# Expert weights in 4 KB pieces, with transposes that pick every fourth (second) column

## The chip, the cores and the metric

One core of one Trainium2 chip runs the whole program. The metric is the device time of one execution in microseconds (us). Lower is better.

## The reference, cut to what matters

A block of 2048 tokens with width H = 512 passes through a time-mixing and channel-mixing layer, and then through a mixture of experts. The change touches the routed experts alone:

```python
E, I = (32, 256)          # 32 experts, inner width 256; H = 512
...
_, topk_idx = jax.lax.top_k(sfc_masked, K)      # K = 4 experts for each token
...
up = jnp.einsum('th,ehi->tei', h, Wu)           # Wu: (32, 512, 256), float32
act = _relu2(up)                                # relu, then squared
routed = jnp.einsum('tei,te,eih->th', act, combine, Wd)   # Wd: (32, 256, 512), float32
shared = _relu2(h @ Wsu) @ Wsd
out = (routed + shared).reshape(orig_shape)
```

The two routed products sum over H (512) and over I (256). A sum may be cut into groups of 128 terms in any way, if both factors are cut in the same way.

## The kernel before, in words

The program has five stages. Stages 1 and 2 are the attention-like layer and its channel mixing, stage 3 the shared expert and the routing, stage 4 the routed experts, and stage 5 the rest of the shared expert and the final sum. All semaphores, buffers and the order of the work on each engine are written out by hand.

**Stage 4** works through slots of 128 tokens that are sorted by expert ("tiles"); this input fills 84 of them. The loop runs over passes of GROUP = 12 tiles, with two tiles in flight (u is the tile's number modulo 2). For a tile:

- GpSimd (POOL) gathers the 128 token rows, 544 floats each, from h_d into a ring of 12 tiles xg (`gather`, L1714).
- TensorE transposes the first 512 columns of xg in four pieces of 128 into PSUM (`tin`, L1535). The tile xg is the stationary operand (weight load) and the 128x128 identity the moving one. ScalarE copies the result to xT4 (L1608).
- TensorE computes the up product (`up`, L1543): four float32 matmuls, each of which sums over 128 of the 512 rows of Wu. Piece c of xT4 meets columns c*256 to (c+1)*256 of wu8, the expert's Wu in SBUF. Each of the four runs in two parts, so there are 8 records for a tile.
- ScalarE applies relu into a4 (L1613), VectorE squares it (L1678), and TensorE transposes it in two pieces of 128 columns (`turn`, L1551). It is split into a high and a low part (L1618, L1682).
- TensorE computes the down product in six fp32r matmuls of 512 columns (`down`, L1558 by way of `split_product`, recorded as L614). The weights for it, wds, are split into high and low from wd8 by ScalarE (`w_hi`, L1624) and VectorE (`w_lo`, L1687), column by column in the order in which they lie.
- ScalarE scales the result into a ring of four tiles yo (`take_y`, L1631), and GpSimd adds its rows by an indirect, accumulating DMA to res_d (even tiles) or shx_d (odd tiles) in HBM (`add_rows`, L1735).

The order on TensorE within a step is: up of tile g, tin of tile g+2, turn of tile g-1, down of tile g-2.

**Waits of the row adds.** `add_rows` for tile g waits until the add of tile g-2, into the same array, has landed. `take_y` for tile g waits until the add of tile g-4, whose ring slot it reuses, has landed. GpSimd issues in the order add, gather, add, gather. So an add that lands late holds GpSimd and then ScalarE, and through ScalarE TensorE.

**Expert weights.** A ring of eight slots, w8, holds one expert each: 1024 floats of Wu and 1024 floats of Wd per partition. SyncE issues two DMAs of 512 KB for an expert (`load`, L1256 and L1258) as soon as the slot is free, that is when the previous owner's last down product is done (`stage4_sync`, L1789 to L1792). The first eight experts are loaded in stage 3. Partition p of the Wu slot holds rows p, 128+p, 256+p and 384+p (four pieces of 1 KB in HBM), and partition p of the Wd slot rows p and 128+p (two pieces of 2 KB). After the last expert SyncE loads hT3, 2 MB with 16 KB for each partition (L1797), for stage 5. SyncE's transfers are on queue q1, those of GpSimd on queue q0, and both share the same 16 DMA engines.

Of the kernel before, what the change touches and what calls it, by code (L numbers as in the profile page):

```python
# [24 lines left out]
P = 128  # L25
T, H = 2048, 512
# [4 lines left out]
C = H // P  # L31
# [4 lines left out]
E, EI, TOPK, GROUPS = 32, 256, 4, 4  # L36
# [37 lines left out]
def program(nc, a, out, scratch):  # L74
# [4 lines left out]
    def sem(name):  # L79
        if name not in sem_names:  # L80
            sem_names[name] = ctx.enter_context(nc.semaphore(name))
        return sem_names[name]

    def at(name, shape, dt, kb):

        return nc.alloc_sbuf_tensor_at(name, shape, dt, offset=SBUF0 + int(kb * KB))

    with ctx:
# [13 lines left out]
        ident = at("ident", [P, P], F, 200.5)  # L102
# [98 lines left out]
        wu8, wd8 = w8[:, :, 0:C * EI], w8[:, :, C * EI:]  # L201
        XRING, YRING = 12, 4
        xg = [at(f"xg{n}", [P, H + E], F, 2.125 * (n % 6) + (186 if n < 6 else 80)) for n in range(XRING)]
        xT4 = at("xT4", [P, 2, C * P], F, 180.5)
        a4 = at("a4", [P, 2, EI], F, 92.75)
# [10 lines left out]
        bank = [ctx.enter_context(nc.psum_tensor(f"bank{i}", [P, 512], F)) for i in range(8)]  # L216
# [392 lines left out]
        def split_product(dst, lhs, rhs, n):  # L609

            parts = [(0, 0), (0, 1), (1, 0)]
            for c in range(n):
                for k, (l, r) in enumerate(parts):
                    i = nc.tensor.matmul(dst, lhs(l, c), rhs(r, c), start=c == 0 and k == 0,  # L614
                                         stop=c == n - 1 and k == 2)
            return i
# [631 lines left out]
        def sp_hTb(sp, b):  # L1248
            sp.dma_start(hTb[:, b % 2].bitcast(F), hT_d[b]).then_inc(sem("hb_in"), 16)

        wu_rows = a["L0_ffn_Wu"].rearrange("e (c p) i -> e p c i", p=P)
        wd_rows = a["L0_ffn_Wd"].rearrange("e (c p) i -> e p c i", p=P)

        def load(sp, e, s):

            sp.dma_start(wu8[:, s].rearrange("p (c n) -> p c n", c=C),  # L1256
                         wu_rows[bass.ds(e, 1)].rearrange("a p c i -> p (a c) i")).then_inc(sem(f"w4_in{s % 4}"), 16)
            sp.dma_start(wd8[:, s].rearrange("p (c n) -> p c n", n=H),  # L1258
                         wd_rows[bass.ds(e, 1)].rearrange("a p c i -> p (a c) i")).then_inc(sem(f"w4_in{s % 4}"), 16)

        def landed(sp, r, s):

# [3 lines left out]
        def first_experts(sp):  # L1266
            sp.wait_ge(sem("wsu_lo1"), 2)
            sp.wait_ge(sem("wsd_lo1"), 2)
            sp.wait_ge(sem("lg_in"), NB)
            sp.wait_ge(sem("xp_st"), 16 * NB)  # L1270
            for s in range(4):
                load(sp, s, s)

        def second_experts(sp):
            for s in range(4):
                landed(sp, 0, s)
            for s in range(4, WSLOTS - 1):
                load(sp, s, s)

        def eighth_expert(sp):  # L1280
            sp.wait_ge(sem("rows_in"), 1)
            sp.wait_ge(sem("share_st"), 16)
            load(sp, WSLOTS - 1, WSLOTS - 1)
# [203 lines left out]
        def passes_of(engine):  # L1487

            return engine.value_load(passes_i[0:1, 0:1], min_val=E // GROUP - 1, max_val=PASSES - 1)
# [3 lines left out]
        def owners(engine, g, n=GROUP):  # L1496

            for k in range(n):
                if k % PACK == 0:
                    word = engine.value_load(owner_i[0:1, bass.ds(g + k, 1)], min_val=0,  # L1500
                                             max_val=(1 << OWNER_BITS * PACK) - 1)
                yield k, (word >> OWNER_BITS * (k % PACK)) & E - 1
# [10 lines left out]
        def x_count(i, t):  # L1513

            return 16 * i + 16 * (t // XRING) + 16

        def first_owners(engine, n):
            return [e for _, e in owners(engine, 0, n)]

        def slot_of(ring, e):  # L1520
            return ring[:, bass.ds(e & WSLOTS - 1, 1)].rearrange("p a n -> p (a n)")

        def up3(pe, i):
            pe_inner_up(pe, N4 + i, i, wsu, lambda s, c: hT3[:, s, c], kc=6)

        def down3(pe, i):
            pe_inner_down(pe, N4 + i, i, NSI - 1, lambda s: wsd[s][:, i], to=2)

        def stage4_tensor(pe, down2):
            def tin(i, t, u):  # L1530
                s = t % XRING
                pe.wait_ge(sem(f"xg_in{s}"), x_count(i, t))
                pe.wait_ge(sem("xt4"), GROUP * i + t + 1)
                for c in range(C):
                    m = nc.tensor.transpose(bank[6 + u][:, c * P:(c + 1) * P], xg[s][:, c * P:(c + 1) * P], ident[:])  # L1535
                m.then_inc(sem("t4"), 1)

            def up(g, u, e):
                pe.wait_ge(sem("win"), e + 1)
                pe.wait_ge(sem("xt4"), g + 3)  # L1540
                pe.wait_ge(sem("r4"), g + 1)
                for c in range(C):
                    m = nc.tensor.matmul(bank[4 + u][:, 0:EI], xT4[:, u, c * P:(c + 1) * P],  # L1543
                                         slot_of(wu8[:, :, c * EI:(c + 1) * EI], e), start=c == 0, stop=c == C - 1)
                m.then_inc(sem("u4"), 1)

            def turn(g, u):
                pe.wait_ge(sem("s4"), g + 1)
                pe.wait_ge(sem("al4"), g + 1)
                for c in range(EI // P):  # L1550
                    m = nc.tensor.transpose(bank[2 + u][:, c * P:(c + 1) * P], a4[:, u, c * P:(c + 1) * P], ident[:])  # L1551
                m.then_inc(sem("at4"), 1)

            def down(g, u):
                pe.wait_ge(sem("al4"), g + 3)
                pe.wait_ge(sem("wl4"), g + 1)
                pe.wait_ge(sem("y4"), g + 1)
                split_product(bank[u][:], lambda s, c: aT4[:, u, s, c * P:(c + 1) * P],  # L1558
                              lambda s, c: wds[:, u, s, c * H:(c + 1) * H], EI // P).then_inc(sem("d4"), 1)

            def step(i, t, e, more=True):
                g, u = GROUP * i + t, t % 2
                up(g, u, e)
                if more:
                    tin(i, t + 2, u)
                turn(g - 1, 1 - u)
                down(g - 2, u)

            down2(NSI - 2)
            pe.wait_ge(sem("owner_in"), 1)  # L1570
            passes = passes_of(pe)
            early = first_owners(pe, 2)
            pe.wait_ge(sem("rows_in"), 1)
            tin(0, 0, 0)
            tin(0, 1, 1)
            down2(NSI - 1)
            pe.wait_ge(sem("kc_free"), N4 + 2)
            up(0, 0, early[0])
            tin(0, 2, 0)
            up(1, 1, early[1])  # L1580
            tin(0, 3, 1)
            pe.wait_ge(sem("sh_in"), (NB - 2) * BT + 1)
            turn(0, 0)
            pe.wait_ge(sem("sh_in"), (NB - 1) * BT)
            with pe.Fori(0, PASSES - 1) as i, pe.If(i < passes):
                for k, e in owners(pe, GROUP * i + 2):
                    step(i, 2 + k, e)
            n = GROUP - 2
            for k, e in owners(pe, GROUP * passes + 2, n):
                step(passes, 2 + k, e, more=k < n - 2)  # L1590
            final = GROUP * passes + GROUP - 1
            pe.wait_ge(sem("hb_in"), 16 * NB)
            turn(final, 1)
            up3(pe, 0)
            down(final - 1, 0)
            up3(pe, 1)
            down(final, 1)
            for i in range(2, NSI):
                up3(pe, i)
                down3(pe, i - 2)  # L1600
            down3(pe, NSI - 2)
            down3(pe, NSI - 1)
# [292 lines left out]
```

## Time and profile before

| | us |
|---|---|
| median of 3 runs (1082.77 to 1088.84) | 1088.8 |
| the profiled execution | 1089.09 |
| its span, first to last instruction | 1086.9 |
| TensorE busy in the span | 1048.4 (96%) |
| first to last up product of stage 4 | 709.4 to 1034.3 |

The profiled execution is one of its own, 0.3 us above the median; 2.2 us of it lie outside the span. In the profile PE is TensorE's matmuls, PEld its weight loads, which run beside the matmul before them, DVE is VectorE, ACT ScalarE, POOL GpSimd and SPq SyncE's queue of instructions. L1543 is line 1543 of the kernel. The ends of matmuls are modelled, so the time from one start to the next says more than the duration of one. A row of the timeline gives the start, the time from the first start to the last end, the engine and line, and the count.

### The profile page before, as it was taken

What the parts mean: (1) busy time and instruction counts of PE and PEld (TensorE: products, weight loads), DVE (VectorE), ACT (ScalarE), POOL (GpSimd) and SP (SyncE); (2) the same over time, 40 slices, a digit from 0 to 9 for tenths busy, and PEclk for the clock granted to TensorE, in tenths of its full rate; (3) what the DMA queues carried; (4) which work ended last, traced back from release to release, by engine and by line L of the source; (5) the groups of instructions that cost most, each with busy time, mean ns of one, the idle gap of its engine ahead of it and who ended that gap; (6) DMA issues with size and microseconds to landing.
All of it is one profiled execution on the core that took longest, in us unless ns stands there. A gap on an engine that the chain in (4) does not pass through costs nothing.

```text
span 1086.9 us, 17057 instructions
## 1 busy us (share of the span) xinstructions
PE 1048.4 (96%) x4868; PEld 841.1 (77%) x4869; DVE 573.4 (53%) x1113; ACT 535.1 (49%) x893; POOL 436.9 (40%) x327
## 2 busy tenths in 40 slices
PE   2999999999999999999999999999999999999998
PEld 0446888888788878887887788888878888887887
DVE  7978947804661475230034796845444444544514
ACT  4644546333333333343344333367767576766742
POOL 1011304221321122112224424467777777887642
PEclk9999999999999999999999999999999999999999
DMA  8705296416422642334266771277989999986678
GB/s 278 265 1 194 86 335 209 166 59 249 155 98 66 224 154 96 116 118 151 90 223 228 259 220 39 68 189 149 279 182 241 254 225 312 199 197 118 87 182 337
DMA packets 98307, 192.91 MB, mean 177 GB/s; under 512 B 13001, under 2 KB 33481, under 8 KB 97745
## 3 DMA queue, kind: packets, MB, share of 16 engines
q1 hardware_dynamic: 79008, 151.63, 40.0%
q0 software_dynamic: 18816, 39.87, 19.6%
q10 hardware_dynamic: 432, 0.79, 0.2%
q8 instruction: 27, 0.44, 0.2%
q14 instruction: 24, 0.19, 0.1%
HBM read 137.78 MB, written 60.03 MB: 182 GB/s over the span
## 4 chain that ended last, share of the span: by engine, by line
PE 75%; DMA 11%; DVE 7%; issue 3%; POOL 2%; SPq 1%; ACT 1%; ACTq 0%; DVEq 0%; POOLq 0%
PE bank L614 35%; PE bank L939 21%; PE bank L1543 8%; DMA shx_d<-yo,idy 6%; PE bank L529 5%; DMA res_d<-yo,idy 3%; PE bank L1535 2%; DVE big L1328 1%; PE bank L1551 1%; DMA hT_d<-hT 1%; SPq L1062 1%; DMA g1b<-in_L_attn_ln_b 1%; PE bank L950 1%; PE bank L1007 1%; PE bank L960 0%
## 5 line engine op out<-in xcount | busy, mean ns | idle before, releaser
L920 POOL TENSOR_TENSOR ksp_lo<-ra,ksp_hi 128x512 fp32r<-128x512 f32 x96 | 148.3, 1545 | 443.0 <-ACT ksp_hi L870 442.9
L1687 DVE TENSOR_TENSOR wds<-w,wds 128x1024 fp32r<-128x1024 f32 x84 | 103.0, 1226 | 167.1 <-ACT wds L1624 167.1
L1543 PE MATMUL bank<-w,xT 128*128 x672 | 159.4, 380 | 1.2 <-ACT xT L1608 0.8
L939 PE MATMUL bank<-vring,ksp_hi 128*128 128x512 f32 x512 | 159.3, 393 | 0.0
L862 ACT ACTIVATE ra<-bank 128x512 f32<-128x512 f32 x96 | 57.4, 597 | 178.2 <-PE bank L614 175.9
L1543 PEld LDWEIGHTS bank<-w,xT 128*128 128x128 f32 x672 | 127.5, 190 | 21.8 <-issue 1.8
L614 PE MATMUL bank<-wds,aT 128*128 128x512 f32 x504 | 138.4, 410 | 0.1
L870 ACT ACTIVATE ksp_hi<-ra 128x512 fp32r<-128x512 f32 x96 | 60.7, 632 | 124.7 <-PE bank L939 124.2
L939 PEld LDWEIGHTS bank<-vring,ksp_hi 128*128 128x128 f32 x512 | 95.5, 188 | 20.1
L1631 ACT ACTIVATE yo<-bank,xg 128x512 f32<-128x512 f32 x84 | 57.8, 688 | 93.1 <-PE bank L614 48.5
L614 PEld LDWEIGHTS bank<-wds,aT 128*128 128x128 f32 x504 | 89.0, 190 | 17.3 <-issue 0.3
L614 PE MATMUL bank<-xcT_hi,wck_lo 128*128 128x512 f32 x256 | 101.7, 397 | 0.0
L614 PE MATMUL bank<-xcT_lo,wck_hi 128*128 128x512 f32 x256 | 101.5, 396 | 0.0
L614 PE MATMUL bank<-xcT_hi,wck_hi 128*128 128x512 f32 x256 | 101.1, 395 | 0.0
L939 PE MATMUL bank<-vring,ksp_lo 128*128 128x512 f32 x256 | 99.7, 390 | 0.0
L1714 POOL DMA_INDIRECT xg<-h_d,idc x60 | 85.0, 1416 | 18.3 <-issue 14.3
L1624 ACT ACTIVATE wds<-w 128x1024 fp32r x84 | 88.2, 1050 | 1.2 <-issue 1.1
L1735 POOL DMA_INDIRECT res_d<-yo,idy x36 | 57.6, 1600 | 31.4 <-DMA res_d<-yo,idy 17.2
L1735 POOL DMA_INDIRECT shx_d<-yo,idy x36 | 58.5, 1625 | 22.3 <-DMA shx_d<-yo,idy 11.7
L370 POOL TENSOR_TENSOR mix_lo<-mx,mix_hi 128x512 fp32r<-128x512 f32 x16 | 20.1, 1289 | 106.3 <-ACT mix_hi L427 106.3
L864 ACT ACTIVATE ra<-ra 128x512 f32<-128x512 f32 x96 | 60.7, 632 | 3.1
L614 PE MATMUL bank<-hTb,wsu_hi 128*128 128x512 f32 x192 | 60.1, 394 | 0.1
(270 smaller groups left out, 1912.2 us busy)
## 6 DMA issues: line engine op xcount, KB each, us to landing
vring<-wcv_d SPq DMA_DIRECT2D x64, 512.0 KB, 3.3
w<-in_L_ffn_Wu SPq DMA_DIRECT2D x32, 512.0 KB, 7.4
w<-in_L_ffn_Wd SPq DMA_DIRECT2D x32, 512.0 KB, 9.7
hT_d<-hT SPq DMA_DIRECT2D x16, 512.0 KB, 3.7
hTb<-hT_d SPq DMA_DIRECT2D x3, 2048.0 KB, 10.8
raw_wcv<-in_L_attn_Wcv SPq DMA_DIRECT2D x4, 1024.0 KB, 7.8
raw_wck<-in_L_attn_Wck SPq DMA_DIRECT2D x4, 1024.0 KB, 9.4
f<-in_L_attn_x SPq DMA_DIRECT2D x4, 1024.0 KB, 6.9
```

What stands on the lines that cost most here:

```text
L614: i = nc.tensor.matmul(dst, lhs(l, c), rhs(r, c), start=c == 0 and k == 0, stop=c == n - 1 and k == 2)
L862: nc.scalar.activation(ra[:, i % 2], bank[kc + i % 2][:], ACT.Relu).then_inc(sem("kc_free"), 1)
L864: nc.scalar.activation(ra[:, i % 2], ra[:, i % 2], ACT.Square).then_inc(sem("sq"), 1)
L870: nc.scalar.activation(ksp[0][:, i % 2], ra[:, i % 2], ACT.Copy).then_inc(sem("khi_in"), 1)
L920: nc.gpsimd.tensor_tensor(ksp[1][:, i % 2], ra[:, i % 2], ksp[0][:, i % 2], ALU.subtract).then_inc(sem("klo_in"), 1)
L939: m = nc.tensor.matmul(bank[to + j][:], ksp[l][:, i % 2, j * P:(j + 1) * P], rhs(r), start=i == 0 and k == 0, stop=i == last and k == 2)
L1543: m = nc.tensor.matmul(bank[4 + u][:, 0:EI], xT4[:, u, c * P:(c + 1) * P], slot_of(wu8[:, :, c * EI:(c + 1) * EI], e), start=c == 0, stop= ...
L1624: nc.scalar.activation(wds[:, u, 0], slot_of(wd8, e), ACT.Copy).then_inc(sem("wh4"), 1)
L1631: nc.scalar.activation(yo[:, t % YRING], bank[u][:], ACT.Copy, scale=xg[t % XRING][:, bass.ds(H + e, 1)]).then_inc(sem("y4"), 1)
L1687: nc.vector.tensor_tensor(wds[:, u, 1], slot_of(wd8, e), wds[:, u, 0], ALU.subtract).then_inc(sem("wl4"), 1)
L1714: pool.indirect_dma_start(out=xg[t % XRING][:], out_offset=None, in_=h_d, in_offset=bass.IndirectOffsetOnAxis(ap=row.bitcast(U32), axis=0) ...
L1735: pool.indirect_dma_start(out=(res_d, shx_d)[u], out_offset=bass.IndirectOffsetOnAxis(ap=row.bitcast(U32), axis=0), in_=yo[:, k % YRING], ...
```

## The change

The number of instructions, their order and their waits stay as they are on every engine. What changes is which rows of Wu and Wd a partition holds, and with them which columns the transposes pick.

- Partition p of the Wu slot holds rows 4p to 4p+3, one piece of 4 KB in HBM. Partition p of the Wd slot holds rows 2p and 2p+1, also one piece of 4 KB. The bytes per DMA stay 512 KB.
- Part c of the up product now sums over rows 4q+c of Wu, so piece c of the transposed tile has to hold columns c, 4+c, 8+c, ... of xg: `tin` reads every fourth float, with 16 bytes between one and the next. In the same way `turn` reads every second float of a4, with 8 bytes between them.

```diff
-        wu_rows = a["L0_ffn_Wu"].rearrange("e (c p) i -> e p c i", p=P)
-        wd_rows = a["L0_ffn_Wd"].rearrange("e (c p) i -> e p c i", p=P)
+        wu_rows = a["L0_ffn_Wu"].rearrange("e (p c) i -> e p (c i)", p=P)
+        wd_rows = a["L0_ffn_Wd"].rearrange("e (p c) i -> e p (c i)", p=P)
 
         def load(sp, e, s):
 
-            sp.dma_start(wu8[:, s].rearrange("p (c n) -> p c n", c=C),
-                         wu_rows[bass.ds(e, 1)].rearrange("a p c i -> p (a c) i")).then_inc(sem(f"w4_in{s % 4}"), 16)
-            sp.dma_start(wd8[:, s].rearrange("p (c n) -> p c n", n=H),
-                         wd_rows[bass.ds(e, 1)].rearrange("a p c i -> p (a c) i")).then_inc(sem(f"w4_in{s % 4}"), 16)
+            sp.dma_start(wu8[:, s], wu_rows[bass.ds(e, 1)].rearrange("a p n -> p (a n)")).then_inc(sem(f"w4_in{s % 4}"), 16)
+            sp.dma_start(wd8[:, s], wd_rows[bass.ds(e, 1)].rearrange("a p n -> p (a n)")).then_inc(sem(f"w4_in{s % 4}"), 16)
...
+                every = xg[s][:, 0:H].rearrange("p (q c) -> p c q", c=C)
                 for c in range(C):
-                    m = nc.tensor.transpose(bank[6 + u][:, c * P:(c + 1) * P], xg[s][:, c * P:(c + 1) * P], ident[:])
+                    m = nc.tensor.transpose(bank[6 + u][:, c * P:(c + 1) * P], every[:, c], ident[:])
                 m.then_inc(sem("t4"), 1)
...
+                every = a4[:, u].rearrange("p (q c) -> p c q", c=EI // P)
                 for c in range(EI // P):
-                    m = nc.tensor.transpose(bank[2 + u][:, c * P:(c + 1) * P], a4[:, u, c * P:(c + 1) * P], ident[:])
+                    m = nc.tensor.transpose(bank[2 + u][:, c * P:(c + 1) * P], every[:, c], ident[:])
                 m.then_inc(sem("at4"), 1)
```

## Rows read from the trace of the kernel before

**Rows 1.** The page: busy time and instructions of each engine, slices

```profile
span 1086.9 us, 17057 instructions
PE 1048.4 (96%) x4868; PEld 841.1 (77%) x4869; DVE 573.4 (53%) x1113; ACT 535.1 (49%) x893; POOL 436.9 (40%) x327
PEclk9999999999999999999999999999999999999999
```

**Rows 2.** Chain of waits, 749 to 757 us: start, length, what

```profile
749.12 1.73 PE bank L1543 x8
752.89 1.73 PE bank L1543 x8
756.66 1.73 PE bank L1543 x8
```

**Rows 3.** Up product in two stretches: us, PE busy (records), clock, DMA share, GB/s

```profile
798.10:934.30 136.20, 64.29 (x273) 1.00 0.98 256
934.30:1032.70 98.40, 47.67 (x200) 0.98 0.76 134
```

**Rows 4.** Chain of waits, 795 to 930 us: head by line, and pieces

```profile
by line: DMA shx_d<-yo,idy 50.6%; issue 13.0%; DMA res_d<-yo,idy 12.4%; PE bank L614 5.3%; PE bank L1543 4.8%; POOL xg L1714 3.4%; ACT wds L1624 1.6%; POOL res_d L1735 1.4%; PE bank L1535 1.3%; POOL shx_d L1735 1.2%; ACT yo L1631 1.1%; PE b
...
802.91 8.44 DMA res_d<-yo,idy
...
912.84 7.62 DMA shx_d<-yo,idy
```

**Rows 5.** Transposes and their weight loads in one step, timeline at 844 us

```profile
843.90 0.57 PEld L1535 LDWEIGHTS bank<-ident,xg 128*128 128x128 f32 x4
844.12 0.60 PE L1535 MATMUL bank<-ident,xg 128*128 128x128 f32 x4
...
844.45 0.25 PEld L1551 LDWEIGHTS bank<-ident,a 128*128 128x128 f32 x2
```

**Rows 6.** The two transposing lines: durations min/median/max in ns, first and last start

```profile
L1535 PEld LDWEIGHTS bank<-ident,xg x336: 138/140/144, 705.5 to 1027.6; 128*128 128x128 f32 x168
L1535 PE MATMUL bank<-ident,xg x336: 271/273/273, 705.7 to 1027.7; 128*128 128x128 f32 x168
L1551 PEld LDWEIGHTS bank<-ident,a x168: 137/141/144, 713.6 to 1036.9; 128*128 128x128 f32 x168
```

**Rows 7.** Weight loads that follow each other closely: timeline at 288, 30 and 96 us

```profile
288.64 0.32 PEld L992 LDWEIGHTS bank<-ident,sgT 32*128 32x128 f32 x4 [0.35 <-issue]
...
30.68 3.54 PEld L566 LDWEIGHTS bank<-tm_b,wv 128*128 128x128 f32 x31 [0.24 <-issue]
...
97.13 1.05 PE L574 MATMUL bank<-onesq,pv 128*128 128x128 f32 x8
```

**Rows 8.** DMA, 621 to 628 us (expert weights alone): packets, queue, MB, share of 16 engines

```profile
DMA packets 2051, 2.61 MB, mean 374 GB/s; under 512 B 80, under 2 KB 1469, under 8 KB 2051
q1 hardware_dynamic: 2051, 2.61, 107.5%
```

**Rows 9.** DMA, 1056 to 1058.5, then 153 to 156.5 us (4 KB pieces alone)

```profile
q1 hardware_dynamic: 289, 1.05, 102.9%
...
q1 hardware_dynamic: 666, 1.33, 102.3%
```

**Rows 10.** DMA, 800 to 930 us: share of 16 engines, and issues with median us to landing

```profile
q0 software_dynamic: 7035, 14.92, 55.0%
q1 hardware_dynamic: 14328, 18.78, 42.6%
...
w<-in_L_ffn_Wu SPq DMA_DIRECT2D x17, 512.0 KB, 8.4
...
shx_d<-yo,idy POOLq DMA_INDIRECT x17, 7.2
res_d<-yo,idy POOLq DMA_INDIRECT x16, 7.4
```

**Rows 11.** DMA, 930 to 965 us (no weights any more)

```profile
q1 hardware_dynamic: 38, 0.06, 0.5%
shx_d<-yo,idy POOLq DMA_INDIRECT x5, 5.1
res_d<-yo,idy POOLq DMA_INDIRECT x5, 5.0
```

**Rows 12.** DMA, 966 to 980 us (the 2 MB of hT3, 16 KB pieces)

```profile
q1 hardware_dynamic: 144, 2.10, 43.1%
hT<-hT_d SPq DMA_DIRECT2D x1, 2048.0 KB, 11.5
res_d<-yo,idy POOLq DMA_INDIRECT x1, 11.6
```

## The prediction, made before the run

> **What bounds the kernel now.** I read the page's busy times first. TensorE is busy 96% of the span, at a granted clock of 0.9 or more in every slice, 2.4 GHz being the upper of its two levels [rows 1]. Whatever is added to TensorE is paid; what is taken from a DMA is worth only as much as TensorE waited for it. The change touches stage 4 alone (and the first loads in stage 3, under TensorE's own work), so the question is how much of stage 4 is waiting.
>
> For that I read the chain of waits by its starts. In undisturbed stretches one tile's up product starts 3.77 us after the one before (749.12, 752.89, 756.66) [rows 2]; there TensorE never waits. From 798.1 to 934.3 us there are 273 records of the up product, 8 for a tile: 34 tiles and the first record of the next [rows 3]. They took 136.2 us, at 3.77 us each they would take 128.2, so TensorE lost 8.0 us there. From 934.3 to 1032.7 us there are 200 records, 25 tiles: 98.4 - 94.3 = 4.1 us lost, nearly all in one gap behind the 2 MB transfer of hT3, which the change leaves alone [rows 3, 12]. (Earlier in the stage nothing is lost beyond the start-up.) So 8.0 us is the most that faster expert weights can give.
>
> What are these 8.0 us waits for? The chain from 795 to 930 us consists to 63% of the landing of row adds (50.6% and 12.4%), single ones of 8.44 and 7.62 us [rows 4]. An add must land before the add two tiles later is issued, so when it takes longer than two tiles' 7.55 us, everything slips. While expert weights are streaming, an add lands in 7.2 to 7.4 us by the median, half of them above that [rows 10]; without them in 5.0 to 5.1 [rows 11]. The sixteen DMA engines are 98% busy there, 55.0% with GpSimd's queue and 42.6% with the weights' queue [rows 3, 10].
>
> **First part: the weights' transfers.** Bytes and number of DMAs stay; the pieces per expert fall from 512 + 256 to 128 + 128. With the weights alone on the engines (1 KB and 2 KB pieces mixed), 2.61 MB took 107.5% of 16 x 7 us = 120.4 engine-us, 46.1 per MB [rows 8]. Pieces of 4 KB cost 102.9% of 16 x 2.5 = 41.2 engine-us for 1.05 MB, 39.2 per MB, and in another place 102.3% of 16 x 3.5 = 57.3 for 1.33 MB, 43.1 per MB [rows 9]. An expert is 1.05 MB, so it costs 48.4 engine-us now and 41.2 to 45.3 then; divided by sixteen engines it saves 0.2 to 0.45 us, and I take 0.33 (11%). The 17 experts loaded between 800 and 930 us save 5.6 us of the sixteen engines' time in a stretch of 130 us.
>
> That is not yet time of TensorE. It counts through the landing of the adds, by two effects of opposite sign.
>
> Less to wait for: during an add of some 7.3 us the weights' queue uses 42.6%, 3.1 us of the sixteen engines, and the add lands 7.3 - 5.05 = 2.25 us later than without them [rows 10, 11]. That is 0.73 us of delay for each us of such traffic. 11% less traffic at the same rate is 0.25 us less delay, 7.05 us for the middle add.
>
> Longer turns: a packet of the add waits behind packets of the other queue on the same engine, and these become two to four times as large. The trace has one case of large pieces: hT3 in 16 KB pieces used 43.1% of 14 us = 6.0 us of the engines, and the add beside it landed in 11.6 us, 6.55 later than a free one: 1.1 us for each us of traffic [rows 11, 12]. At 4 KB I expect something between 0.73 and 1.1; by the steps of size it lies nearer to the small pieces, and I take 0.85. Then the delay is 3.1 x 0.89 x 0.85 = 2.3 us, which is what it is now. The two effects cancel.
>
> The Trainium skill has a rule for this turn-taking ("DMA: Bandwidth & Descriptors", Queues, rings and completion order): an engine goes round the queues and drains one whole packet before it switches. The one case in the trace agrees in direction (1.1 against 0.73 us of delay for each us); by the page alone the larger piece would favour the weights at the adds' expense, which is the third rival below.
>
> Bounds of this part: at best all 8.0 us go. At worst the factor is 1.1: the delay is 3.1 x 0.89 x 1.1 = 3.0 us, an add lands 0.75 us later, and each of the 16 pairs of adds in the stretch takes that much longer: + 12 us. Since the engines also get 5.6 us back, I lean a little to a gain and take -1.0 us. The rest of the loads are hidden: those before 700 us lie under the shared expert's matmuls, and `landed` was never late enough to show in the step's pace.
>
> **Second part: TensorE's strided weight loads.** The tile is the stationary operand, so the new pattern is read by the weight load and not by the matmul. 336 loads of xg read with 16 bytes from float to float, 168 loads of a4 with 8 bytes [rows 6]. The trace of before has no strided load of float32, so this has to be bounded.
>
> The load runs beside the matmul before it. Four transposes take 0.60 us and the last lasts 0.273, so the pace is (0.60 - 0.273) / 3 = 0.109 us, set by the moving identity [rows 5, 6]. How long does a load hold its path? Where the moving part is short, four such transposing loads of 128 columns take 0.32 us with 0.136 for one (my reading of the single records): (0.32 - 0.136) / 3 = 0.061 us each [rows 7]. So a load has 0.109 - 0.061 = 0.048 us of cover. Loads that hold the path longer are there too: 31 plain float32 loads in 3.54 us, 0.114 us each, with one moving column; and where such loads meet a moving part of 128 columns, eight matmuls take 1.05 us, (1.05 - 0.273) / 7 = 0.111 us each [rows 7]. A load that takes nearly twice as long as now therefore sets a pace of 0.111 instead of 0.109 us.
>
> The lower bound is nothing, since the number of columns and bytes is the same. The nearest row is the 0.111: 336 x 0.002 = 0.7 us, or 1.0 us if a4's loads were to slow as well. The upper bound is a load that takes four times as long, 4 x 0.053 = 0.213 us: 336 x (0.213 - 0.109) = 35 us for xg alone, 52 us with a4. I take the doubling for xg and nothing for a4, + 0.7 us, and an exposed first load behind the 18 late squares, under 0.1 us.
>
> The Trainium skill speaks against this part ("SBUF — State Buffer", Door 1: The DMA port swizzle, the note on cachelines): SBUF is read in lines of 16 bytes, full speed needs at least two hits on a line, and a new line at each access pays a penalty. a4 with 8 bytes keeps two hits, xg with 16 bytes has one. The same note says that four fp32 may be strided for free, so it does not decide the case, and it gives no size; no run here shows one yet.
>
> **The sum**, against the profiled execution's own time: 1089.1 - 1.0 + 0.7 = 1088.8 us. That execution stands 0.3 us above the median of the three runs shown, whose spread is 6 us, so the same sum for the median is 1088.5.
>
> **The rivals.**
> 1. *The adds come free in time.* If the time given back to the engines counts in full and longer turns do not, the middle add lands at 7.0 us and few exceed 7.55. For it: 98% busy engines. Against it: the 16 KB case. It gives at most 8.0 us: 1082 us. Chance 0.20; 0.03 of it for a gain over 1%, since 10.9 us is more than the waits contain.
> 2. *The strided load is slow* (the slower side). Mechanism: the weight load of xg takes more than 0.109 us and becomes what sets the pace of the transposes. It decides from a bit above twice the present 0.053 to 0.061 us. At three times, 0.165 us, it costs 336 x 0.056 = 19 us: 1108. At four times 35 us: 1124. For it: full use of TensorE, nothing else covers it. Against it: nothing but the cover of 0.048 us. By the skill's line rule (a penalty at each new line) this is where it would bite. Chance 0.13.
> 3. *Longer turns delay the adds.* The worst case of the first part, + 12 us: 1101 us. For it: the 11.6 us add beside hT3. Against it: 4 KB is a quarter of that piece and there are 11% less of engine time. Chance 0.07, half of it over 1%.
> The change does what it says: one piece of 4 KB in HBM and in SBUF for a partition; that it is not packed so has no chance worth a number.
>
> **The numbers.** The forecast, within 3 us of before, has 0.60. A measurement of this kernel can tell about 1% (10.9 us) from no change. Faster by over 1%: 0.03. Slower by over 1%: 0.13 + 0.03 = 0.16. Within 1%: 0.81. The range goes from 1080 (all of the waits gone and a little spread of the runs) to 1102 (the third rival's end); it leaves out most of the second rival, some 0.13.
>
> **What would show it.** In the profile of the changed kernel the packets of the page must fall by 32 x 512 = 16384 from 98307. Weight loads of L1535's successor should last 140 to 200 ns and its matmuls start 0.109 to 0.112 us apart; 0.16 or more is rival 2. The loads of a4 should stay at 141 ns. A step should stay at 3.77 to 3.78 us where TensorE does not wait. In the stretch with weights the adds should land in 7.0 to 7.5 us by the median; 8 or more is rival 3, 6.5 or less rival 1. The forecast is wrong if the step's pace grows by over 0.1 us, or the waits of TensorE in that stretch leave the range of 4 to 12 us.

## The result, and the profile after

The changed kernel takes 1090.39 us by the median of 20 runs (1087.07 to 1095.09), the kernel before in the same series 1085.35 us (1078.91 to 1088.84). The ratio is 1.0050, 95% interval 1.0037 to 1.0063: slower by 5.4 us, 4.0 to 6.8. Both kernels spread over 8 to 10 us from run to run, which matters below: one profile cannot show a difference of 3 us in waits. The execution of before whose rows the prediction read (1089.09 us) is longer than all 20 of these and 3.7 us above their median.

The page's first lines and its count of packets, to set beside [rows 1] and the 98307 packets of before:

```profile
span 1088.6 us, 17057 instructions
PE 1054.5 (97%) x4868; PEld 853.6 (78%) x4869; DVE 574.9 (53%) x1113; ACT 535.8 (49%) x893; POOL 443.3 (41%) x327
...
DMA packets 81922, 192.91 MB, mean 177 GB/s; under 512 B 13000, under 2 KB 17096, under 8 KB 81360
```

As many instructions as before and 16385 packets fewer, so the pieces are packed as the change says. TensorE is busy 6.1 us longer, and its weight loads 12.5 us. Not all of the 6.1 us is the change: near the start, from 20 to 50 us, the mean granted clock was 0.89 in this profile and 0.94 in that of before, in work that the change does not touch.

The strided lines (min/median/max in ns; L1534 was L1535), beside [rows 6]:

```profile
L1534 PEld LDWEIGHTS bank<-ident,xg x336: 195/207/213, 704.2 to 1029.3; 128*128 128x128 f32 x168
L1534 PE MATMUL bank<-ident,xg x336: 272/283/286, 704.4 to 1029.4; 128*128 128x128 f32 x168
```

```profile
L1551 PEld LDWEIGHTS bank<-ident,a x168: 194/209/219, 712.4 to 1038.7; 128*128 128x128 f32 x168
```

The loads went from 140 to 207 ns, those of a4 with 8 bytes from 141 to 209. One step in the chain of waits (start, length, what), beside [rows 2]:

```profile
748.33 1.73 PE bank L1542 x8
750.05 0.47 PE bank L1534 x4
750.52 0.24 PE bank L1551 x2
750.76 1.38 PE bank L614 x6
752.14 1.73 PE bank L1542 x8
```

From 748.33 to 752.14 is one step; the median over the stage is 3.820 us against 3.773. The products keep 1.73 and 1.38 us. The transposes take 0.47 and 0.24 us. 84 steps of 0.047 us more are 3.9 us of TensorE.

The two stretches of [rows 3], in the same form (34 tiles, then 25):

```profile
797.80:934.90 137.10, 64.35 (x273) 1.00 0.94 253
934.90:1034.40 99.50, 47.56 (x200) 0.98 0.74 133
```

34 steps of 3.82 us are 129.9 us, so 7.2 us were lost to waits in the stretch with weights (8.0 before) and 99.5 - 95.5 = 4.0 behind hT3 (4.1 before). But 8.0 is the figure of one long execution. The control below, which is the kernel before with one idle instruction more on SyncE, took 1083.11 us when it was profiled, and its 34 tiles took

```profile
796.60:929.02 132.42, 64.30 (x273) 1.00 0.99 262
```

so it lost 4.1 us to waits there. Over both stretches together, 59 steps, eight kept profiles with contiguous transposes and pieces of 1 or 2 KB (before among them) lost 4.7 to 12.2 us, 7.9 by the median; the three with all weights in 4 KB pieces lost 11.2 us (this one), 10.2 (the loads alone) and 10.9 (the interleaved one). The start of stage 4 moved as well, between 708.0 and 712.9 us, whatever the form of the loads. These two make the spread from run to run.

The queues from 800 to 930 us, beside [rows 10]:

```profile
DMA packets 12203, 33.62 MB, mean 259 GB/s; under 512 B 2057, under 2 KB 2057, under 8 KB 12203
...
q0 software_dynamic: 7037, 14.82, 56.2%
q1 hardware_dynamic: 5166, 18.80, 39.3%
```

The weights' queue fell from 42.6% to 39.3% of 130 us, 4.3 us of the sixteen engines. That time was saved, and the kernel is still slower.

### The profile page after: what moved, and what is told of

It is laid out like the page before. It is cut to its first block, busy times and chain, and to the rows that moved or that the text cites. A ratio compares the mean times of both kernels' runs of the same rounds, so it can differ in the third digit from the quotient of the medians.

```text
span 1088.6 us, 17057 instructions
## 1 busy us (share of the span) xinstructions
PE 1054.5 (97%) x4868; PEld 853.6 (78%) x4869; DVE 574.9 (53%) x1113; ACT 535.8 (49%) x893; POOL 443.3 (41%) x327
## 4 chain that ended last, share of the span: by engine, by line
PE 78%; DVE 7%; issue 6%; DMA 5%; POOL 1%; ACT 1%; SPq 1%; DVEq 1%; ACTq 0%; POOLq 0%
PE bank L614 35%; PE bank L939 21%; PE bank L1542 8%; PE bank L529 6%; DMA res_d<-yo,idy 2%; PE bank L1534 2%; PE bank L1551 1%; DMA hT_d<-hT 1%; DVE big L1326 1%; DMA g1b<-in_L_attn_ln_b 1%; SPq L1062 1%; PE bank L950 1%; DMA shx_d<-yo,idy 1%; PE bank L1007 1%; DVE a L1678 1%
## 5 line engine op out<-in xcount | busy, mean ns | idle before, releaser
L939 PEld LDWEIGHTS bank<-vring,ksp_hi 128*128 128x128 f32 x512 | 95.5, 188 | 20.1
```

Of the source, the lines that this page charges most:

```text
L939: m = nc.tensor.matmul(bank[to + j][:], ksp[l][:, i % 2, j * P:(j + 1) * P], rhs(r), start=i == 0 and k == 0, stop=i == last and k == 2)
```

## The experiments

Two causes are possible for 5.4 us: theory 1, the strided weight loads on TensorE; theory 2, 4 KB pieces that make the row adds land late. The first four runs separate them. In all of them the kernel before ran beside on the same chip.

**Loads alone.** The new `load` with contiguous transposes; tile columns and weight rows are then paired differently from the reference, which leaves the routed product another one.

```diff
-                    m = nc.tensor.transpose(bank[6 + u][:, c * P:(c + 1) * P], every[:, c], ident[:])
+                    m = nc.tensor.transpose(bank[6 + u][:, c * P:(c + 1) * P], xg[s][:, c * P:(c + 1) * P], ident[:])
...
-                    m = nc.tensor.transpose(bank[2 + u][:, c * P:(c + 1) * P], every[:, c], ident[:])
+                    m = nc.tensor.transpose(bank[2 + u][:, c * P:(c + 1) * P], a4[:, u, c * P:(c + 1) * P], ident[:])
```

> The expert weights come in 4 KB pieces, but both transposes read contiguous columns as before (the columns of the tile and the rows of the weights are then paired wrongly; the instructions and their times are those of a real run). Theory 1 (the strided weight loads of TensorE cost the time): a step outside waits is back at 3.77 us, the weight loads of the transposes last 140 ns, and the kernel is no slower than before: 0 to 3 us faster, since the weights' queue uses some 4 us less of the sixteen engines. Theory 2 (4 KB pieces make the row adds land later): slower than before by 3 to 5 us, with over 11 us of waits in the step list.

Measured: 1089.18 us against 1086.10, ratio 1.0028 (1.0010 to 1.0047), slower by 3.0 us (1.1 to 5.1), with a step of 3.773 us and loads of 140 ns. TensorE's instructions are those of before, so this loss comes with the pieces, as theory 2 has it. The waits in its one profile, expected at over 11 us, do not show where:

```profile
800.30:935.00 134.70, 64.32 (x273) 1.00 0.95 257
```

34 steps of 3.773 are 128.3, so 6.4 us were lost there, between the 4.1 of the control and the 8.0 of before. The medians of 12 and 35 runs, not the single profiles, carry the verdict.

**Strides alone.** The strided transposes with the loads of before, paired differently too.

```diff
-        wu_rows = a["L0_ffn_Wu"].rearrange("e (p c) i -> e p (c i)", p=P)
-        wd_rows = a["L0_ffn_Wd"].rearrange("e (p c) i -> e p (c i)", p=P)
+        wu_rows = a["L0_ffn_Wu"].rearrange("e (c p) i -> e p c i", p=P)
+        wd_rows = a["L0_ffn_Wd"].rearrange("e (c p) i -> e p c i", p=P)
```

> The transposes read every fourth (second) column, the expert weights are loaded in 1 KB and 2 KB pieces as before (again paired wrongly, on purpose of the measurement of time alone). Theory 1: a step outside waits takes 3.82 us, weight loads last 195 to 213 ns, and the kernel is slower than before by 4 us (84 x 0.047) or a little more than the changed kernel is. Theory 2: no slower than before by more than 1 us.

Measured: 1087.41 us, ratio 1.0009 (0.9994 to 1.0023), + 1.0 us (-0.7 to 2.5), with a step of 3.820 us and loads of 207 and 209 ns. TensorE works 3.9 us longer, but less than that arrives at the end. Theory 1 had expected 4 us, and the run with one more transpose below takes this up. Taken from the 5.4 us of the whole change, the strides alone leave 4.4 us for the pieces (an estimate of about 2.3 to 6.5 from the two intervals), a second sign of their cost beside the run with the loads alone.

**One side at a time.** Both of these compute what the reference does. The first, shown in the edit, has Wu in 4 KB pieces and every fourth column of xg, the second Wd in 4 KB pieces and every second column of a4; each leaves the other side as before.

```diff
-        wd_rows = a["L0_ffn_Wd"].rearrange("e (p c) i -> e p (c i)", p=P)
+        wd_rows = a["L0_ffn_Wd"].rearrange("e (c p) i -> e p c i", p=P)
...
-                    m = nc.tensor.transpose(bank[2 + u][:, c * P:(c + 1) * P], every[:, c], ident[:])
+                    m = nc.tensor.transpose(bank[2 + u][:, c * P:(c + 1) * P], a4[:, u, c * P:(c + 1) * P], ident[:])
```

> Only the up side of the change: Wu in 4 KB pieces and every fourth column of xg; Wd and a4 as before. Theory 1: the four transposes of xg cost their part of the 47 ns, some 30 ns for a tile (the first of them is still covered by the up product's long matmul), 2.5 us in all, less a small gain from the DMA: 1.5 to 3 us slower than before. Loads of xg 195 to 213 ns, of a4 140. Theory 2: half of the 5 us at the least, and more if 1 KB to 4 KB matters more than 2 KB to 4 KB.

Measured: ratio 1.0030 (1.0009 to 1.0051), + 3.3 us, step 3.806 us.

> Only the down side: Wd in 4 KB pieces and every second column of a4; Wu and xg as before. Theory 1 with a cost that depends on the 8 or 16 bytes: if two floats to a line of 16 bytes were free as I assumed, the loads of a4 would last 141 ns and nothing is lost. By the profile of the changed kernel they will last about 195 to 215 ns and cost some 15 to 20 ns for a tile, 1.3 to 1.7 us in all. Theory 2: less than 1 us, since 2 KB to 4 KB changes the turns least.

Measured: ratio 1.0015 (0.9998 to 1.0033), + 1.6 us, step 3.787 us; the interval just holds no change. The two together make 0.45%, the whole change 0.50%. The up side costs 33 ns of the step and the down side 14 ns. The loads of a4, two floats to every 16 bytes, are slow too (197 ns).

**The two prices by themselves.** A program that leaves the whole computation out and measures strided loads and single row adds.

> A program of its own that leaves the whole computation out (its output is a copy of x) and measures the two disputed prices alone. TensorE: float32 weight loads of 128 columns with 1, 2, 3, 4, 8, 16 and 31 floats from one to the next, before transposes that move 32 columns (so that the load sets the pace), before transposes of 128 columns, and before plain matmuls of one column. DMA: 36 accumulating row adds of 128 rows, one at a time, six each beside nothing and beside 2 MB of expert weights in pieces of 512 B, 1, 2, 4 and 16 KB. Theory 1 (the load holds its path for twice as long when strided): pace 0.060 us at 1, about 0.12 at 2 and at all larger strides; with 128 moving columns 0.109 and then 0.12. Theory 2 (longer turns): the add lands in 4.2 to 5 us beside nothing, and later with each step of the piece's size, by about 1 us from 1 KB to 4 KB and more at 16 KB. If piece size does not matter, all five streams give the same landing within 0.3 us.

Transposes with 32 moving columns, where the load sets the pace, first with 1 float from one to the next; then transposes of 128 columns with 2, 3 and 4. Length of 16, TensorE busy (records; those that reach over an edge are counted twice), clock:

```profile
39.42:40.44 1.02, 1.01 (x16) 1.00 0.50 191
```

```profile
54.93:56.84 1.91, 1.91 (x18) 1.00 0.30 17
56.84:58.67 1.83, 1.83 (x18) 1.00 0.81 124
58.67:60.61 1.94, 1.94 (x18) 1.00 0.05 10
```

A contiguous load holds its path for about 62 ns (start to start of the single records), as I had read from [rows 7]. With 2 floats it is 120 ns, with 3 113, with 4 121, and with 8, 16 and 31 floats between 112 and 123. So the load takes nearly twice as long, whatever the stride, and it is this, not the moving identity's 109 ns, that sets the pace. Theory 1's price is confirmed.

The adds by themselves: 4.81 us to landing beside nothing, and by the median of six 6.80, 8.68, 8.55, 8.77 and 8.33 us beside 2 MB in pieces of 512 B, 1, 2, 4 and 16 KB. The first and the last two of these rows, as the median of six:

```profile
res_d<-yo,rows_i POOLq DMA_INDIRECT x6, 4.8
...
res_d<-yo,rows_i POOLq DMA_INDIRECT x6, 8.8
...
res_d<-yo,rows_i POOLq DMA_INDIRECT x6, 8.3
```

From 1 KB up a single add beside one burst does not care for the size (0.4 us in all); the 512 B stream was issued in eight DMAs over a longer time and differs in more than its pieces. This went against theory 2, which had expected 1 us more from 1 to 4 KB. It also takes away the meaning that the prediction gave to its 11.6 us beside hT3 [rows 12]: beside the same 2 MB in the same 16 KB pieces a single add landed in 8.33 us, so what made that one so late is not shown.

**One more transpose.** To see what becomes of TensorE's extra time.

```diff
-                for c in range(C):
+                for c in (0, *range(C)):
                     m = nc.tensor.transpose(bank[6 + u][:, c * P:(c + 1) * P], xg[s][:, c * P:(c + 1) * P], ident[:])
```

> The kernel before with one transpose of xg issued twice in each tile: 109 ns more of TensorE in each of 84 steps, 9.2 us in all, and nothing else. Theory A (a slower step lets the row adds land in time, so part of added TensorE work is taken out of the waits): step 3.88 us, waits fall to about half, and the kernel is slower by 4 to 6 us. Theory B (TensorE is the bound and all of it is paid): slower by 9 us.

Measured: ratio 1.0036 (1.0015 to 1.0057), + 3.9 us (1.6 to 6.2) for 84 x 0.104 = 8.7 us more of TensorE (step 3.877 us). The stretch with weights:

```profile
804.70:937.65 132.95, 64.20 (x273) 1.00 0.96 258
```

34 steps of 3.877 are 131.8 us: 1.1 us of waits are left, where the profile of before had 8.0 and that of the control 4.1. Against the control the stretch is only 0.5 us longer, though its steps alone are 3.5 us longer. That is theory A. I read it so: an add has two steps to land in, and when the step is longer, more adds land in time. By the medians the waits give back 4.8 of the 8.7 us (2.5 to 7.1), about half. So a longer step costs less than its own length here, which fits the strides alone with 1.0 (up to 2.5) of 3.9 us.

**Wd in 1 KB pieces**, twice, and three relatives: Wd in the same 2 KB pieces but in two DMAs of 256 KB (twice), everything in 1 KB pieces and four DMAs, and a control with one idle instruction on SyncE.

```diff
-            sp.dma_start(wd8[:, s].rearrange("p (c n) -> p c n", n=H),
-                         wd_rows[bass.ds(e, 1)].rearrange("a p c i -> p (a c) i")).then_inc(sem(f"w4_in{s % 4}"), 16)
+            for h in range(2):
+                sp.dma_start(wd8[:, s].rearrange("p (c h n) -> p h c n", h=2, n=H // 2)[:, h],
+                             wd_rows[bass.ds(e, 1), :, :, h * (H // 2):(h + 1) * (H // 2)].rearrange("a p c i -> p (a c) i")).then_inc(sem(f"w4_in{s % 4}"), 16)
```

> The kernel before with Wd loaded in 1 KB pieces too, as two DMAs of 256 KB for each expert (halves of the rows), so all of an expert comes in 1 KB pieces. Theory 2 (longer pieces delay the adds): faster than before by 0.5 to 1.5 us, although the engines move 1 KB pieces some 9% slower than 2 KB pieces. Theory 3 (not the size, but the engines' time decides): slower by 0 to 1 us.

> The kernel before with one instruction that does nothing behind each expert's two loads on SyncE. All theories expect no change: within 0.15% of before. If it moves by 0.25% or more, differences of 3 us between kernels of this program come from where its code lies, and say nothing on pieces.

> The kernel before with Wd loaded in the same 2 KB pieces, but as two DMAs of 256 KB. Theory 2 (size of the piece): no change, within 0.15%. Theory 4 (shorter DMAs): faster by 2 to 3 us, like the run with Wd in 1 KB pieces, which also used two DMAs of 256 KB.

> The kernel before with each expert in four DMAs of 256 KB, all in 1 KB pieces; transposes as before. Theory 2: like the run with Wd in 1 KB pieces, faster than before by 1 to 3 us. Theory 4: faster still, by 3 to 5 us.

> The run with Wd in 2 KB pieces and two DMAs of 256 KB once more, since its interval (-0.35% to +0.05%) held both theories. Theory 2: within 0.15% of before. Theory 4: faster by 0.15 to 0.3%.

> The run with Wd in 1 KB pieces once more, since the model shows no gain of 1 KB over 2 KB and the run with everything in 1 KB pieces none either. If its 0.27% were real, faster by 0.1 to 0.4% again; by the model within 0.15% of before.

| run | ratio to before | 95% interval |
|---|---|---|
| Wd in 1 KB pieces | 0.9973 | 0.9957 to 0.9989 |
| the same again | 0.9995 | 0.9972 to 1.0017 |
| all in 1 KB pieces, four DMAs | 1.0003 | 0.9985 to 1.0020 |
| Wd in 2 KB pieces, two DMAs | 0.9985 | 0.9965 to 1.0005 |
| the same again | 0.9986 | 0.9965 to 1.0006 |
| control | 1.0003 | 0.9981 to 1.0024 |

The first run's gain did not come back although its interval did not hold 1. The loads alone rest on one such series of 12 runs too; what backs them are the whole change, the model and the 8 KB run below. The control's one instruction moved nothing beyond its interval of 0.2% either way. Below 4 KB neither the size nor the number of the DMAs gives a gain that can be told for certain; Wd in two DMAs came out 0.15% faster both times, each interval just holding 1. None of these is a proven improvement on the kernel before, and neither theory's gain of 1 us or more from four DMAs in 1 KB pieces came.

**Interleaving.** The changed kernel with the xg transposes laid between the up matmuls.

```diff
+                for c in range(C):
+                    m = nc.tensor.matmul(bank[4 + u][:, 0:EI], xT4[:, u, c * P:(c + 1) * P],
+                                         slot_of(wu8[:, :, c * EI:(c + 1) * EI], e), start=c == 0, stop=c == C - 1)
+                    k = nc.tensor.transpose(bank[6 + u][:, c * P:(c + 1) * P], every[:, c], ident[:])
+                m.then_inc(sem("u4"), 1)
+                k.then_inc(sem("t4"), 1)
```

> The changed kernel, with the four transposes of xg laid between the four up matmuls, so that each strided load runs beside a matmul of 216 ns instead of one of 109. Theory 1: the loads of xg keep 195 to 213 ns but the step goes from 3.820 to about 3.79 us (the turn of a4 still pays its part), and the kernel gets 0.5 to 2 us faster than the changed one, still slower than before. If instead the step stays at 3.82, the strided load costs more than the time in which it holds the path.

Measured: step 3.793 us, ratio to before 1.0032 (1.0010 to 1.0054). Its lines for xg:

```profile
L1556 PEld LDWEIGHTS bank<-ident,xg x320: 195/197/231, 717.6 to 1030.2; 128*128 128x128 f32 x160
L1556 PE MATMUL bank<-ident,xg x320: 272/273/421, 717.8 to 1030.4; 128*128 128x128 f32 x160
```

The loads are still strided and long (197 ns), but the matmuls are back at 273 ns and 27 of the 47 ns of the step are gone: what a strided load costs is the time by which it outlasts the matmul beside it, here one of 216 ns. As expected its median ratio lies between the changed kernel and before; but the gain on the changed kernel, 0.18%, was not measured against it directly, and the two intervals overlap, so that gain in time is not shown.

**A model of stage 4's transfers.** A program with the adds, the gathers, the loads at the kernel's steps and the waits between them, and no products.

> A program of its own that keeps only stage 4's transfers and their waits (all products are left out): TensorE counts steps of 3.76 us, GpSimd adds and gathers one tile in each step, TensorE stops if the add six tiles back has not landed, and SyncE loads 18 experts at the steps at which the kernel loads them from tile 24 to 59. Nine stretches of 36 steps: as before (1 KB and 2 KB), 4 KB, Wd in 1 KB (three DMAs), Wd in 2 KB but in two DMAs of 256 KB, none, and the four again in reverse. Theory 2 (larger pieces delay the adds in bursts of loads): the stretches with 4 KB lose 2 to 4 us more than those as before, those with 1 KB lose 1 to 3 us less. Theory 4 (not the size of a piece but the DMAs of 256 KB helped the run with 1 KB): both three-DMA forms lose the same, less than before. If neither matters, all four differ by under 1 us and the 3 us of the runs come from elsewhere.

A stretch that followed an empty one, or came first, took as long as the empty one (135.6 us), so what a stretch inherits counts as much as its own pieces. Leaving these out, the 36 steps took longer than that by 8.6 and 10.9 us with 4 KB, 8.0 and 6.9 with Wd in 1 KB, 7.2 with Wd in two DMAs, 6.3 as before (once). So 4 KB lost 2.3 to 4.6 us more than before, as theory 2 had it, but Wd in 1 KB lost no less than before. The next two runs give each form two stretches and read the second.

> The model of stage 4's transfers again, with the expert's 1 MB in both halves alike: 72 steps each of 1 KB, 2 KB and 4 KB pieces in two DMAs, 8 KB pieces in one, and 2 KB and 1 KB pieces in four DMAs of 256 KB. Read from the second 36 steps of each. Theory 2 (size of the piece): the loss per 36 steps rises from 1 and 2 KB to 4 KB by 2 to 3 us and further at 8 KB; two or four DMAs make no difference at the same size. Theory 4 (length of the DMA): the forms with four DMAs lose 1 us less or more than those with two.

> The same in reverse order, so that what a stretch inherits from the one before it is turned round. Same expectations; a difference that keeps its sign in both counts.

Second stretches in the first order, 36 steps each: 1 KB, 2 KB, 4 KB, 8 KB, then 2 KB and 1 KB in four DMAs. Length, TensorE busy (records), clock, DMA share, GB/s:

```profile
209.75:352.65 142.90, 138.43 (x1245) 1.00 1.00 269
497.55:640.30 142.75, 137.91 (x1244) 1.00 0.99 270
787.65:935.55 147.90, 140.01 (x1244) 0.99 0.95 261
1096.15:1255.35 159.20, 140.38 (x1244) 0.99 0.91 242
1399.55:1542.45 142.90, 137.45 (x1244) 1.00 0.99 270
1683.65:1829.00 145.35, 138.72 (x1244) 1.00 1.00 268
```

and of the reverse order 8 KB, 4 KB, 2 KB and 1 KB:

```profile
800.05:955.25 155.20, 139.96 (x1245) 0.99 0.92 247
1102.35:1249.45 147.10, 139.22 (x1245) 1.00 0.97 261
1392.25:1535.15 142.90, 137.20 (x1245) 1.00 0.98 268
1679.25:1822.40 143.15, 138.62 (x1243) 1.00 1.00 271
```

The same work takes 143 us with 1 or 2 KB (once 145), 147 to 148 with 4 KB and 155 to 159 with 8 KB, in both orders; the step from 2 to 4 KB is 4 to 5 us where 2 to 3 were expected. Four DMAs in place of two make no steady difference (143 and 145 us here, 143.3 and 143.5 in the reverse order); 8 KB pieces came in one DMA for each expert, so there size and number were not parted. And the DMA share falls as the time rises (0.99 with 2 KB, 0.95, 0.91): share times length is 141, 141 and 145 us of the engines, so with large pieces the time is lost mostly in waiting and not in the engines' work. Where a row has a granted clock of 0.99, it stood at 0.50 for one stretch of 3.4 us, which explains 1.7 us at most; the 147.10 of 4 KB has none. That is theory 2, the size of the piece, in the steady stream.

**8 KB and 2 KB in the whole kernel.** Contiguous transposes; the 8 KB run loads two neighbouring matrices of Wu in place of the expert's Wu and Wd, the 2 KB run pairs Wu's rows differently from the tile's columns, so the routed product is another one in both.

```diff
-        wu_rows = a["L0_ffn_Wu"].rearrange("e (c p) i -> e p c i", p=P)
+        wu_pairs = a["L0_ffn_Wu"].rearrange("(g m) (q c) i -> g (m q) (c i)", m=2, c=8)
...
+            sp.dma_start(w8[:, s], wu_pairs[bass.ds(e & 15, 1)].rearrange("a p n -> p (a n)")).then_inc(sem(f"w4_in{s % 4}"), 16)
```

> The kernel before, with each expert's 1 MB as one DMA of 8 KB pieces (two neighbouring matrices of Wu in place of the expert's Wu and Wd, so the product is another one; transposes contiguous). By the isolated model, where 8 KB pieces lost 12 to 16 us more than 1 or 2 KB in 36 steps with 18 loads: slower than before by 10 to 18 us, with a step outside waits of 3.77 us and the loss in the bursts of loads. If piece size matters in the model alone: within 3 us of before.

Measured: 1099.73 us (median of 4 runs) against 1086.26, ratio 1.0121 (1.0069 to 1.0174), + 13 us.

```profile
800.00:946.65 146.65, 66.10 (x273) 0.98 0.89 235
```

34 steps of 3.773 are 128.3 us, so 18.4 us were lost where before lost 8.0 and the control 4.1. Two stretches of 3.4 us with the lower clock, behind waits, are in it; this is one:

```profile
833.20:836.60 3.40, 3.40 (x10) 0.54 0.64 101
```

At 0.50 each costs 1.7 us at most, so 15 us remain that are waits.

> The kernel before with Wu in 2 KB pieces (two neighbouring rows in a partition, two pieces), Wd in 2 KB as before, contiguous transposes (paired wrongly for Wu). By the model, where 1 and 2 KB lose the same: within 0.15% of before, so that the 3 us of 4 KB pieces come between 2 and 4 KB.

Measured: ratio 0.9999 (0.9978 to 1.0020). So the whole kernel follows the model: nothing from 1 to 2 KB (within 0.2%), 3 us at 4 KB (1.1 to 5.1), 13 us at 8 KB.

## Why the prediction was wrong

The forecast was a change of - 0.3 us, within 3 us of before, at 1088.5 us. The change is a real loss of 5.4 us, and both terms of the sum were wrong. That the measured 1090.39 us lies only 1.9 us above the forecast is luck: the sum started from an execution 3.7 us above the median of before. From 1085.35 it would have given 1085.05. The signs that were to call the forecast wrong did not see it either (the step grew by 0.047 and not by over 0.1 us, the waits stayed at 7.2 us), but four smaller ones failed: loads of 207 instead of 140 to 200 ns, 209 instead of 141 for a4, 0.118 to 0.122 us apart instead of 0.109 to 0.112, a step of 3.820 us instead of 3.77 to 3.78. And this series tells 1.4 us, not 10.9, from no change.

- **What bounds the kernel** held in kind: stage 4, with waits behind row adds. The size of 8.0 us did not: it belongs to one long execution, and the control, the same work on TensorE and the same transfers, had 4.1.
- **The first part, the weights' transfers** (- 1.0 us): the saving of engine time was there (5.6 us forecast, 4.3 seen), but the step that failed is the balance of the two effects. I weighed less traffic against longer turns with a factor of 0.85 us of delay per us of traffic at 4 KB, and let them cancel; the loads alone cost 3.0 us (1.1 to 5.1). The third rival had the sign and got a chance of 0.07; its + 12 us did not come at 4 KB. The way of reckoning, one add's delay for each us of traffic, failed too: a single add beside a burst took 8.77 us with 4 KB and 8.68 with 1 KB pieces, and the row behind the factor of 1.1, the 11.6 us beside hT3, was not met again with the same pieces alone (8.33 us). The cost shows only where adds, gathers and loads follow each other in a steady stream, in the kernel and in the model of it.
- **The second part, the strided loads** (+ 0.7 us): the doubling I assumed is what happens (62 to 120 ns). The term that was mis-sized is its consequence. I took the pace of 0.111 us from a row of another kind of load that was "nearly twice as long"; twice my own 0.061 would have been 0.122, so the sum went against my own reading. The real one is 0.118 to 0.122 for most of the six transposes, because the load holds the path for 0.120 and the cover of 0.048 us was 0.011 too short. And the exemption of a4 was wrong. Together 3.9 us of TensorE instead of 0.7. Rival 2 named this mechanism (0.13), with prices of 19 us and more that did not come.
- **The sum**: "whatever is added to TensorE is paid" is false in this kernel. Of 8.7 us added, 3.9 arrived (1.6 to 6.2). So 3.0 us for the pieces and 1.0 us (up to 2.5) for the strides make the 4.0 to 6.8 of the whole; their single intervals add to 0.4 to 7.6, so the split is not known more finely.
- The Trainium skill's note on cachelines ("SBUF — State Buffer", Door 1: The DMA port swizzle) let me exempt a4: two hits on a 16-byte line should be full speed. For weight loads the rows disagree, 209 ns with 8 bytes and 207 with 16. For the moving operand they agree: 114 ns with 8 bytes, 172 with 12, 227 with 16 (last section). Its other sentence, four fp32 for free, agrees with neither. Here the measurement decides. The Trainium skill's rule on turns ("DMA: Bandwidth & Descriptors", Queues, rings and completion order), by which an engine drains a whole packet of one queue before it goes to the next, agrees in direction with the losses of 3.0 us at 4 KB and 13 us at 8 KB, but not with the single adds, which did not care for the size; and its packet is a group of descriptors, while each piece here is one packet of the profile.

What stays open is the route of theory 2 in detail, and no profile shows in which waits of the whole kernel the 3.0 us at 4 KB lie. A single add beside one burst did not land later with 4 or 16 KB pieces; only the steady stream of adds, gathers and loads loses. Which queue's packet waits for which there was not resolved. A version with 4 KB pieces and contiguous transposes through a permuted store of h was not tried; by the loads alone I expect it to be slower than before.

## What to carry to other kernels

Larger contiguous pieces save DMA engine time, but where a short transfer of another queue is on the path, they can cost more in its wait than they save: ask who shares the engines before asking how full they are. A strided float32 weight load costs the time by which it outlasts the matmul beside it, so put it beside a long one. Where the bound engine also waits for a fixed latency, added work on it is only partly paid; that saved work is then only partly earned I would expect, but no run here took work away. And a bound on waits that is read from one profile (8.0 us here, 4.1 in another) needs the spread of the runs beside it.

## What the runs showed that I had not expected

- A float32 load of 128 columns with any stride from 2 to 31 floats holds its path for 110 to 123 ns, against 62 contiguous; 3, 8 and 16 floats were a little quicker (110 to 114) than 2, 4 and 31 (120 to 123).
- Plain one-column float32 matmuls, whose contiguous loads are paced at 111 to 112 ns in the probe, were paced at 116 to 118 ns with 2 floats, in the few starts before the granted clock fell to 0.50 (from then on 213 to 239, where nothing contiguous stands beside them). So a load that is slow anyway may lose little by its stride; so few starts leave it unsure.
- That stretch of the program in which the granted clock had fallen to 0.50 gave the same pace for the strided loads (110 to 123 ns with 8, 16 and 31 floats) as the one at 1.00 (112 to 123): these strided loads were not paced by TensorE's clock.

```profile
46.09:47.85 1.76, 1.76 (x18) 0.50 0.52 93
...
49.62:51.48 1.86, 1.86 (x18) 0.50 0.41 30
```

```profile
60.61:62.41 1.80, 1.80 (x18) 1.00 0.33 18
...
64.22:66.07 1.85, 1.85 (x18) 1.00 0.01 1
```

The first pair are 16 transposes of 32 columns with 8 and with 31 floats at 1.2 GHz, the second 16 of 128 columns with the same strides at 2.4 GHz.

- A stride in the moving operand is another matter. The probe ends with plain float32 matmuls of 128 columns (two records each) whose weights are contiguous and whose moving operand is strided. At a granted clock of 1.00 their starts are 111 to 112 ns apart with 1 float, 114 with 2, 172 with 3 and 227 with 4; with 8, 16 and 31 floats they are 233, 218 and 230. So in the moving operand 8 bytes cost 2 to 3 ns and 16 bytes cost 115, where in the weight load both cost 11 to 12 beside a matmul of 109. By these rows `tin`, whose stride lies in the stationary operand, has it on the cheap side. With 2, 3 and 4 floats:

```profile
94.13 1.99 PE L142 MATMUL bank<-wide 128*128 128x128 f32 x16
...
96.82 2.92 PE L142 MATMUL bank<-wide 128*128 128x128 f32 x16
...
100.45 3.79 PE L142 MATMUL bank<-wide 128*128 128x128 f32 x16
```
